# Cross-attention: the router's logits as one transposed product, and another order of residuals, low parts and bias on VectorE

## The reference

```
x = layernorm(x + self_attention(x))                 # 16 heads of 32
x = layernorm(x + cross_attention(ctx, x))           # queries from x, keys and values from ctx:
                                                     # 77 rows per batch, 8 heads of 64
x = layernorm(x + experts(x))                        # top 1 of 8 experts, 512 -> 2048 -> 512
```

```
logits = x_flat @ router_w.T                         # 4096 x 8
probs = softmax(logits); chosen_e = argmax(probs); chosen_p = max(probs)
pos = rank of the token among those with its expert; kept = pos < 768
buf[chosen_e, pos] = x ; eo = w2 . gelu(w1 . buf + b1) + b2
y = eo[chosen_e, pos] * chosen_p * kept
```

## Time and profile before

| | us |
|---|---|
| median of three runs | 3785.6 |
| the profiled execution's own time | 3778.94 |
| its span | 3777.2 |
| TensorE busy | 3470.1 (92%) |
| VectorE busy | 2519.5 (67%) |
| ScalarE busy | 1754.4 (46%) |
| GpSimd busy | 2045.9 (54%) |

### The profile page before, as it was taken

One profiled execution on the slowest core, in us unless ns is written; L12 is line 12 of the kernel. 1 busy time (PEld: TensorE's weight loads), 2 busy tenths in 40 slices (PEclk: granted clock), 3 DMA queues, 4 the chain that ended last, 5 costly groups with the idle time before them and its releaser, 6 DMA issues. The chain is left out here.

```text
span 3777.2 us, 51836 instructions
## 1 busy us (share of the span) xinstructions
PE 3470.1 (92%) x18133; PEld 2274.6 (60%) x18134; DVE 2519.5 (67%) x4522; ACT 1754.4 (46%) x3098; POOL 2045.9 (54%) x1031
## 2 busy tenths in 40 slices
PE   7999999999999999999999858899869889899985
PEld 5455455455454554554544336788758778788874
DVE  6777777777777777777777336788634755466566
ACT  2555555555555555555555533343323433343343
POOL 2789898888988898888898820011110100110112
PEclk9999999999999999999999878999879999999998
DMA  6321322313122223223110032222132422232332
GB/s 219 95 62 55 93 63 66 98 48 97 57 65 85 66 67 91 64 66 99 48 40 12 7 98 74 81 82 77 65 114 71 136 88 97 95 104 100 118 117 99
DMA packets 190735, 309.76 MB, mean 82 GB/s; under 512 B 25609, under 2 KB 72329, under 8 KB 190490
## 3 DMA queue, kind: packets, MB, share of 16 engines
q1 hardware_dynamic: 164330, 238.58, 20.3%
q0 software_dynamic: 15072, 45.89, 3.5%
q10 hardware_dynamic: 11088, 22.02, 1.7%
HBM read 197.23 MB, written 61.33 MB: 68 GB/s over the span
## 5 line engine op out<-in xcount | busy, mean ns | idle before, releaser
L463 DVE TENSOR_REDUCE sa_part_max<-sa_mx 128x1 f32<-128x512 f32 x2048 | 1281.9, 680 | 541.5 <-PE sa_mx L574 537.4
L426 ACT ACTIVATE sa_prob<-sa_sc 128x512 f32<-128x512 f32 x2048 | 1122.0, 595 | 822.5 <-PE sa_sc L620 780.8
L247 POOL TENSOR_TENSOR sa_quad_sum<-sa_quad_sum,sa_prob 128x1024 f32<-128x1024 f32 x512 | 1207.6, 2404 | 7.7 <-ACT sa_prob L426 7.7
L574 PE MATMUL sa_mx<-sa_k_stack,sa_q_stack 96*128 96x512 f32 x2048 | 967.2, 474 | 27.1 <-DVE sa_part_max L463 15.8
L620 PE MATMUL sa_sc<-sa_q_stack,sa_k_stack 98*128 98x512 f32 x2048 | 864.6, 424 | 8.2 <-ACT sa_prob L426 8.2
L247 POOL TENSOR_TENSOR sa_quad_sum<-sa_prob 128x1024 f32<-128x1024 f32 x256 | 616.1, 2429 | 256.1 <-ACT sa_prob L426 256.1
L574 PEld LDWEIGHTS sa_mx<-sa_k_stack,sa_q_stack 96*128 96x128 f32 x2048 | 389.4, 190 | 377.1 <-issue 205.0
L620 PEld LDWEIGHTS sa_sc<-sa_q_stack,sa_k_stack 98*128 98x128 f32 x2048 | 389.1, 190 | 318.8 <-ACT sa_prob L426 273.6
L1856 PE MATMUL ex_h<-ex_xT,ex_w 128*128 128x384 f32 (+2 forms) x2688 | 467.6, 330 | 81.9 <-issue 35.0
L1856 PEld LDWEIGHTS ex_h<-ex_xT,ex_w 128*128 128x128 f32 x2688 | 450.7, 196 | 106.4 <-issue 77.8
L589 PE MATMUL sa_pv<-sa_prob,sa_v 128*32 128x512 f32 x4096 | 501.9, 608 | 0.7 <-ACT sa_prob L426 0.7
(11 more groups left out here) (201 smaller groups left out, 3397.1 us busy)
## 6 DMA issues: line engine op xcount, KB each, us to landing
ex_w_in<-in_L_ffn_w_dram SPq DMA_DIRECT2D x130, 512.0 KB, 4.3
sa_xT<-xT SPq DMA_DIRECT2D x57, 1024.0 KB, 5.1
sa_q_stack<-sa_hilo SPq DMA_DIRECT2D x372, 64.0 KB, 2.0
sa_k_stack<-sa_hilo SPq DMA_DIRECT2D x360, 64.0 KB, 2.0
ex_xg<-rows POOLq DMA_DIRECT2D x54, 256.0 KB, 3.2
rows<-sa_empty SPq DMA_DIRECT2D x48, 257.0 KB, 3.8
ex_rows<-rows POOLq DMA_DIRECT2D x8, 1542.0 KB, 7.5
sa_prob<-in_x_dram ACTq DMA_DIRECT2D x8, 1024.0 KB, 7.4
```

The costliest lines, as they stand in the source:

```text
L247: pool.tensor_tensor(quad_sum[:, i % 2, heads, :], so_far, prob[:, k, heads, :], ALU.add).then_inc(quad_ready, 1)
L426: act.activation(prob[:, kt % 4, j, :], sc[n % 2][:, :], ACT.Exp, scale=SCALE).then_inc(prob_ready, 1)
L463: dve.reduce_max(part_max[:, q, j, k:k + 1], mx[n % 3][:, :], AX_X).then_inc(max_read, 1)
L574: pe.matmul(mx[n % 3][:, :], q_stack[0:QK, j, at:at + P], k_stack[0:QK, g // NQ % 2, j, k * BANK:(k + 1) * BANK], start=True, stop=True).t ...
```

## The change

The router's weights become the stationary operand. Four products of 512 columns (one per k) give the logits transposed, 8 experts on partitions and 512 tokens as columns, in bank 6. ScalarE copies them into a new buffer `lgT` (8 x 512) with `leave_logits`, after `leave_p(n, 1)`. TensorE transposes them, four times 8 x 128 into 128 x 8, to the same place in bank 7 as before, with `transpose_logits` between `transpose_p(n, 3)` and `transpose_x1n(n+1)`; in the tail it follows the product at once. The semaphore counts are adapted: `lg_mm` is raised twice per chunk, `x2T_ready` five times.

On VectorE the order within a chunk changes: `residual2(n, 0)` and `low_p(n, 2)` come ahead of `place_tokens(n-2)`, `low_p(n, 3)` follows this directly and comes ahead of `residual2(n, 1)`, and `add_bias(n+2)` moves from before the residuals to between those of tiles 2 and 3.

```diff
+        lgT = s.sb("lgT", [E, BANK])
+        LEFT = KC + 1
+        LG_MM = 2
# VectorE
-                dve.wait_ge(lg_mm, n + 1)
+                dve.wait_ge(lg_mm, (n + 1) * LG_MM)
                 low_p(n, 1)
                 if more:
                     norm1(n + 1)
+                residual2(n, (0,))
+                low_p(n, 2)
                 if n >= 2:
                     place_tokens(n - 2)
-                if n + 2 < NCH:
-                    add_bias(n + 2)
-                residual2(n, (0,))
-                low_p(n, 2)
+                low_p(n, 3)
                 residual2(n, (1,))
-                low_p(n, 3)
                 if n > 0:
                     choose(n - 1)
                 if more:
                     leave_x1nT(n + 1)
                 if n == PER_B - 1:
                     low_qk()
-                residual2(n, (2, 3))
+                residual2(n, (2,))
+                if n + 2 < NCH:
+                    add_bias(n + 2)
+                residual2(n, (3,))
                 variances(n, 1)
# ScalarE
             def leave_x2T(n):
-                act.wait_ge(lg_mm, n)
+                if n > 0:
+                    act.wait_ge(lg_mm, (n - 1) * LG_MM + 1)
+            def leave_logits(n):
+                act.wait_ge(lg_mm, n * LG_MM + 1)
+                act.activation(lgT[:, :], bank[6][0:E, :], ACT.Copy).then_inc(x2T_ready, 1)
                 for t in range(TQ):
                     leave_p(n, t)
+                    if n > 0 and t == 1:
+                        leave_logits(n - 1)
...
+            leave_logits(NCH - 1)
# TensorE
-                        pe.wait_ge(x2T_ready, (n - 1) * KC)
+                        pe.wait_ge(x2T_ready, (n - 1) * LEFT)
...
             def route_logits(n):
-                pe.wait_ge(x2T_ready, (n + 1) * KC)
+                pe.wait_ge(x2T_ready, n * LEFT + KC)
+                for k in range(KC):
+                    last = pe.matmul(bank[6][0:E, :], rw[:, k, :], x2T[:, k, :], start=(k == 0), stop=(k == KC - 1))
+                last.then_inc(lg_mm, 1)
+
+            def transpose_logits(n):
+                pe.wait_ge(x2T_ready, (n + 1) * LEFT)
                 if n > 0:
                     pe.wait_ge(route, (n - 1) * ROUTE_STEPS + RANKS_READ)
                 for t in range(TQ):
-                    for k in range(KC):
-                        last = pe.matmul(bank[7][:, t * E:(t + 1) * E], x2T[:, k, t * P:(t + 1) * P], rw[:, k, :], start=(k == 0), stop=(k == KC - 1))
+                    last = pe.transpose(bank[7][:, t * E:(t + 1) * E], lgT[:, t * P:(t + 1) * P], ident[0:E, 0:E])
                 last.then_inc(lg_mm, 1)
...
                 transpose_p(n, 3)
+                if n > 0:
+                    transpose_logits(n - 1)
                 if n + 1 < NCH:
                     transpose_x1n(n + 1)
...
             route_logits(NCH - 1)
+            transpose_logits(NCH - 1)
             rank(NCH - 1)
```

More of the change, by code:

```diff
@@ L1473, in transpose_x2 @@
                     pe.wait_ge(x2_ready, (n + 1) * TQ)
-                pe.wait_ge(x2T_ready, n * KC + k)
+                pe.wait_ge(x2T_ready, n * LEFT + k)
                 for t in range(TQ):
```

## The result

The changed kernel took 3754.7 us (median of 4 runs, 3752.7 to 3755.1), the kernel before, run between them, 3785.7 (4 runs, 3783.7 to 3788.8): a ratio of 0.992, 95% interval 0.9908 to 0.9932, so 31 us faster. The forecast was 3748 in a range of 3741 to 3767. The result lies within it, but just above the 3743 to 3754 that the prediction gave to its own case, without a rival. Further runs of the same two files gave 3751.6 (0.9916) and 3785.5 (1.0006).

A forecast was written before the change was run, and what follows sets the result against it. TensorE in its own order was taken to bound the cross-attention stage, losing time to waits and a low clock. Savings over chunks 0 to 7 and the tail summed to 37.4 us, subtracted from 3785.6: 3748, range 3741 to 3767.

The forecast's parts named there:

- The clock: At `outputs(n, 0)`: 512-column products hold the clock, so it takes 3.6 us everywhere; 1.6 to 2.7 back in chunks 2 to 6.
- rivals 1 and 2: Clock rivals: eight weight columns do not hold it (3767, chance 0.15); the longer transpose run lowers it (3759, chance 0.08).
- rival 2: From transposes of p to `outputs(n, 2)`, four more transposes lower the clock: 1.6 us per chunk, 11 in all; chance 0.08.
- The product: The router's product on TensorE: eight records replace 32 and take 3.5 us, so TensorE's own time there stays.
- Rival 4: Clock stays low from transposes of x2 to next scores, streaming product doubles: 9 us per chunk, 3811; chance 0.03.
- The waits at x1n: TensorE before `transpose_x1n`: 6.95 us lost ahead of tile 1 in chunk 2 becomes a wait of 0.45 at tile 3.
- The step on VectorE's order: VectorE's sequence through one chunk, with the bias's wait for its rows gone; a plain chunk takes 49.2 us.
- Chunks 1 to 3, 5 and 6: Savings forecast for these chunks: 6.4, 10.0, 3.6, 7.4 and 1.6 us.
- Chunk 4: VectorE starts 2.1 us late; scores wait 1.0 and tile 3 of x1n 1.2: 52.0 us, 2.2 saved.
- Chunk 0: The two waits at x1n, 2.3 us in all, shrink to 0.2: 2.1 saved.
- Chunk 7: Clock comes up halfway through the product, which ends after 5.2 us; `outputs(7, 0)` takes 3.6: 3.7 saved (2.5 to 4.3).
- Rival 3: VectorE becomes the bound in chunks 1 to 6, each giving 2 us back, at scores or tile 3: 3760; chance 0.07.

The follow-up runs named there:

- e3_after_again: The changed kernel run and profiled once more with no edit; 3751.6 us, ratio 0.9916.
- e6_product_twice: The changed kernel with the router's four products of 512 columns issued twice, result the same; 3781.4 us, ratio 0.9995.
- second pair: Profiles from running the kernel before and the changed kernel once more, both with no edit; 3785.5 and 3751.6 us.
- before again: The kernel before run and profiled once more with no edit; 3785.5 us, ratio 1.0006.
- e1_order_only: The kernel before with VectorE's new order alone, keeping the old product of 8 moving columns; 3756.5 us, ratio 0.993.

## Why the prediction was right, and by what it missed

- *The clock* (rivals 1 and 2): as forecast. With the product of 8 weight columns `outputs(n, 0)` ran at 1.00 and took 3.6 everywhere, and the clock was 1.00 through chunks 1 to 6. In e3_after_again it fell once in them, to 0.97 over chunk 4, behind the 2.1 us for which the scores wait for the keys. The longer run, 3.7 us from the transposes of p to `outputs(n, 2)`, stayed at 1.00 too. The Trainium skill's rule on transposes ("TensorE: Matmul & The Clock Gate", Part 4), the reason given for rival 2, cost nothing here.
- *The product*: 3.53 us for eight records against 3.5 taken in proportion to columns. Rival 4 rested on nothing in the trace being this product; e6_product_twice shows 3.44 us for each further one. One reading in that rival was wrong: it says that a product bound by weight loads does not double at the low clock, but the old one took 7.00 us at 0.50 in the tail against 3.49. In the tail the new one took 5.96 (5.2 forecast) at a mean clock of 0.60.
- *The waits at x1n*: 6.95 became 0.62 in chunk 2 (0.45 forecast). The step on VectorE's order left out residual 0's wait for the store of the output rows, 1.12 us: with the bias gone from in front of it, the residual meets a buffer that the DMA still reads. The bias itself waited for nothing, as said.
- *Chunks 1 to 3, 5 and 6*: 6.5, 9.5, 3.5, 7.2 and 1.5 (second pair 7.2, 9.6, 4.7, 7.6 and 1.5) against 6.4, 10.0, 3.6, 7.4 and 1.6. The wait for the keys was 2.10, as was said (2.4). Plain chunks took 49.3 to 49.7, against 49.2.
- *Chunk 4*: it took 53.2 us, not 52.0. The step counted waits of 1.0 at the scores and 1.2 at tile 3, which were 0.77 and 0.83, and put at nothing the wait for ScalarE's copy of x2T, which stands behind the high parts of vw: 1.75. The gain was 1.0 instead of 2.2, and 2.7 in the second pair, where the old kernel was slower in this chunk.
- *Chunk 0*: 2.1 forecast, 0.4 in the first pair of profiles, 1.3 in the second. Its waits at x1n fell from 2.3 to 0.47, near what the step says, but its earlier part differs by more than that from one execution to the next (74.2 to 81.5 over all kernels).
- *Chunk 7*: 4.5 against 3.7 in the first pair, a loss of 1.4 in the second: the old kernel's clock there is chance, and that 4.5 came near 3.7 was luck.
- *The failed step*: "The stage ends in a barrier before the experts, so this goes to the end in full; the experts are unchanged." The stage's 34.2 did arrive at the barrier, but the experts were not unchanged. Four profiles with the old product have 1014.3 to 1019.6 us of experts (mean 1016.2). The seven with the new product issued once and no padding have 1018.4 to 1025.9 (mean 1022.5), so the two groups overlap by one. TensorE's waits by issue and for `ex_w` together, which replace each other, are 46.7 to 47.5 us in the former and 49.6 to 54.0 in the latter; the padded two have 44.8 and 44.3. So 6 us of gain are given back on average, 10 in the first profile. That 320 instructions put back ahead of the experts take the loss away, the two padded kernels show, with the padding in different places, and the waits by issue at the same places in all kernels bear it out. Why is open: that it goes by where the experts' code lies in the stream was only argued, as no other amount of padding was tried. And e6_product_twice does not fit in full: it has 128 of the 320 back and waits by issue of only 31.8 us, but 1026.8 us of experts, with TensorE busy for 897 us instead of 887 to 891.

The result is 6.7 us over the forecast. In the second pair of profiles the stage falls 4.7 short of the forecast gain and the experts take 2.0. The first pair has 3.2 and 10.3, and the execution of before in it ran 6.7 under its median. No pair is one of medians, so neither is an exact division of the 6.7. Rival 3 came closest in kind (VectorE sets tile 3 in chunks 2 to 6), but at 0.3 to 0.8 us.

## What to carry to other kernels

When a wait and a low clock stand in the same stretch, the clock's gain counts only once the wait is gone: price them in that order, not as a sum. Move a wait for a DMA behind the work that others wait for, and fill an engine's remaining wait with work nobody needs soon, as `place_tokens` does. When a change takes some hundred instructions out of a long program, look at the waits by issue in the stages behind it as well, above all where these branch; here useless instructions, put partly into a wait, were worth 10.3 us, and a finer order on ScalarE nothing that the time resolves.

## What was not expected of the hardware

- TensorE's waits by issue in an untouched stage moved by 13 us (40.1 to 26.8) with 160 transposes and their weight loads more in front of it, those for `ex_w` by 4 the other way (13.2 to 17.5), and the whole kernel by 10.3.
- The clock's fall behind the old product is not fixed: in the seven chunks of before and before again and of e1_order_only, `outputs(n, 0)` took 3.6 us in one, one and three of them, and 5.0 to 6.4 in the others; behind the new product it took 3.6 in all, in every kernel.
- A weight load of 8 columns took 85 to 137 ns, median 90, where one of 128 (the experts' second product) took 190 on the mean. The Trainium skill ("TensorE: Matmul & The Clock Gate", LDWEIGHTS) says that the time goes by columns; here it falls with them, but far less than in proportion. The loads of 128 columns and 8 rows for the transposes of logits took 133 to 139, so columns alone do not settle it.
